# Side jobs of the first attention: scatter and gathers spread over the steps, eight tiles turned at a time, one spare-bank job a step

## The reference, cut to what matters

```
u, v, q, k = split(silu(xn @ W1 + b1), 4)          # 16 heads of 64
av = (silu(q k^T) / 2048) v                        # no softmax: silu of the scores
s  = layernorm(av * u, gamma, beta) @ W2 + b2
```

## Time and profile before

| | us |
|---|---|
| three runs: lowest, median, highest | 4219.31, 4656.99, 4722.14 |
| the profiled execution, its own time | 4205.8 |
| its span (slowest core, core 4) | 4204.2 |
| spans of the eight cores | 4160.4 to 4204.2 |
| TensorE busy in the span | 3919.9 (93%) |
| ScalarE busy | 2097.0 (50%) |
| VectorE busy | 1634.2 (39%) |
| attention of layer 0, core 4 | 129 to 789 |

### The profile page before, as it was taken

One profiled execution on the slowest core, in us unless ns is written; L12 is line 12 of the kernel. 1 busy time (PEld: TensorE's weight loads), 2 busy tenths in 40 slices (PEclk: granted clock), 3 DMA queues, 4 the chain that ended last, 5 costly groups with the idle time before them and its releaser, 6 DMA issues.

```text
span 4204.2 us, 55884 instructions; the slowest of 8 cores (4160.4 to 4204.2 us)
## 1 busy us (share of the span) xinstructions
PE 3919.9 (93%) x20362; PEld 1681.0 (40%) x20362; DVE 1634.2 (39%) x1775; ACT 2097.0 (50%) x2027; POOL 413.6 (10%) x684
## 2 busy tenths in 40 slices
PE   6799777799899999999999999999999999999999
PEld 3333232344444433344443344444344434433444
DVE  6485411002563435333244434424453342355421
ACT  4799757620450556443355554525654553467101
POOL 3000110101110000001100000020000002100000
PEclk9999988999899999999999999999999999999999
DMA  5466865845443349998433333343333334333794
GB/s 157 79 106 109 120 96 105 126 74 152 144 159 128 130 127 220 218 218 212 144 126 123 112 132 117 137 152 113 122 131 124 122 122 145 133 115 119 230 302 143
DMA packets 146591, 593.24 MB, mean 141 GB/s; under 512 B 22517, under 2 KB 49429, under 8 KB 102677
## 3 DMA queue, kind: packets, MB, share of 16 engines
q0 software_dynamic: 80960, 448.84, 41.5%
q1 hardware_dynamic: 65370, 140.83, 10.3%
HBM read 637.80 MB, written 120.63 MB: 180 GB/s over the span
## 4 chain that ended last, share of the span: by engine, by line
PE 76%; DMA 8%; ACT 8%; issue 4%; DVE 3%; DVEq 2%; POOL 0%; SPq 0%; ACTq 0%; POOLq 0%
PE psP L1697 37%; PE psP L1663 10%; PE psP L1719 5%; ACT pt L786 4%; PE psP L1465 3%; PE psP L1413 3%; PE psP L929 3%; PE psP L987 3%; PE psP L1291 2%; DMA w2s<-W 2%; PE psP L291 2%; DVEq L153 1%; PE psP L779 1%; PE psP L312 1%; DMA wsl<-h2wt 1%
## 5 line engine op out<-in xcount | busy, mean ns | idle before, releaser
L1697 PE MATMUL psP<-hB,wsl 128*128 128x512 bf16 x4096 | 923.3, 382 | 23.1 <-DMA wsl<-h2wt 14.2
L1697 PE MATMUL psP<-hA,wsl 128*128 128x512 bf16 x4096 | 928.8, 381 | 3.7 <-DVE nrm L1337 3.7
L1489 DVE TENSOR_TENSOR accs<-accs,pt 128x2048 f32<-128x2048 f32 x192 | 440.1, 2292 | 897.7 <-ACT pt L1480 897.6
L1697 PEld LDWEIGHTS psP<-hB,wsl 128*128 128x128 bf16 x4096 | 393.9, 98 | 524.5 <-issue 77.4
L1697 PEld LDWEIGHTS psP<-hA,wsl 128*128 128x128 bf16 x4096 | 389.4, 98 | 509.3 <-issue 67.8
L1480 ACT ACTIVATE pt<-psP,nbias 128x1024 bf16<-128x1024 f32 x512 | 542.6, 1111 | 93.6 <-PE psP L1465 86.7
L786 ACT ACTIVATE pt<-psP 128x2048 bf16<-128x2048 f32 x341 | 476.6, 1449 | 80.2 <-PE psP L779 76.4
L1663 PE MATMUL psP<-xn,wsl 128*128 128x512 bf16 x2048 | 452.0, 379 | 3.5 <-ACT sgt L1139 1.8
L1480 ACT ACT_TABLE_LOAD x200 | 256.6, 1283 | 355.8 <-PE psP L1465 338.0
L1704 ACT ACT_TABLE_LOAD x181 | 232.2, 1283 | 259.9 <-PE psP L1697 257.1
L1663 PEld LDWEIGHTS psP<-xn,wsl 128*128 128x128 bf16 x2048 | 199.1, 98 | 242.1 <-issue 7.6
(11 more groups left out here) (229 smaller groups left out, 3243.1 us busy)
## 6 DMA issues: line engine op xcount, KB each, us to landing
wsl<-h1b POOLq DMA_DIRECT2D x125, 1024.0 KB, 5.1
wsl<-h2b POOLq DMA_DIRECT2D x96, 1024.0 KB, 5.1
h1b<-h1wt POOLq DMA_DIRECT2D x32, 1024.0 KB, 11.1
wsl<-h2wt POOLq DMA_DIRECT2D x32, 1024.0 KB, 13.7
h2b<-wsl SPq DMA_DIRECT2D x32, 1024.0 KB, 13.3
wsl<-w1b POOLq DMA_DIRECT2D x96, 256.0 KB, 3.6
wsl<-w2b POOLq DMA_DIRECT2D x96, 256.0 KB, 4.1
wsl<-w3b POOLq DMA_DIRECT2D x24, 1024.0 KB, 5.3
```

Source lines behind the costliest of these rows:

```text
L1489: VI(lambda v, a=a, sl=sl: v.tensor_tensor(accs[:], a[:], pt2[sl][:], OP.add))
L1697: emitter(lambda t, it=it, i=i, b=b, src=src: t.matmul(pb(b), wsl[i][:, it, :], src[:, it, :], start=(it == 0), stop=(it == 31)))
```

## The change

- The last row operation now signals, and the first two tiles of W2 are asked for behind it, ahead of the write of `dest_d`.
- The 16 scatters follow at one a step, each behind a wait of POOL for the matmuls of its step; a `w2_sum` comes after every second one. Before, the eight sums came first, one a step, and all scatters were emitted with the last.
- The eight gathers are emitted one a step in the same way.
- `heavy_turn` transposes eight tiles into the whole of bank 7 and copies 1024 columns at once; there are eight calls instead of 16. The means come after them.
- The loop takes at most one job that uses bank 7 in a step, and none in a step in which a fill used it.

```diff
         for i, f in enumerate(row_ops):
             yield (0.3 if i == 3 else 4.5 if i in (5, 10) else 2.5), 0
             VD()
-            VN(f)
+            (VN if i < len(row_ops) - 1 else VI)(f)
+
+        w2_load(tok(cv))
+        w2_load(None)
...
-        w2_load(tok(cv))
-        w2_load(None)
-        for j in range(8):
-            yield 0, 3
-            yield 2.8, 0
-            w2_sum(j)
-        k_accW[0] = tok(cv)
-        wk("v", k)
-        VI(lambda v: v.tensor_scalar(hdi[:], desti[:], NHEAVY, None, OP.min))
+        yield 0, 8
         wk("g", k)
         qtab = stream("qtab")
         for tt in range(NTT):
+
+            yield 0, 4
+            wk("g", tok(ct))
             qtab.n += 16
             Q["g"].append(lambda g, tt=tt: g.indirect_dma_start(
                 tab_d, bass.IndirectOffsetOnAxis(desti[:, tt:tt + 1], 0), tokid[:, tt:tt + 1], None
                 ).then_inc(qtab.h, 16))
+            if tt % 2 == 1:
+                yield 2.8, 0
+                w2_sum(tt // 2)
+        k_accW[0] = tok(cv)
+        wk("v", k)
+        VI(lambda v: v.tensor_scalar(hdi[:], desti[:], NHEAVY, None, OP.min))
         k_rows = tok(cv)
         wk("y", tok(qtab))
         k = y_words(stream("qr10"), sidx[:], tab_d[0:NHEAVY, :].rearrange("(t p) o -> p (t o)", p=128))
-        yield 0, 16
+        yield 0, 10
         wk("g", k, k_rows)
         wk("g", *[tok(st) for st in qxr])
         qxg = stream("qxg")
         for st in range(8):
+            yield 0, 4
+            wk("g", tok(ct))
             qxg.n += 16
...
         k_gather[0] = tok(qxg)
+        yield 0, 8
+        for c in range(NCH):
+            yield 0.8, 0, 1
+            heavy_turn(c)
         for f in range(2):
             yield 0.7, 0, 1
             w2_mean(f)
-        yield 0, 16
-        for c in range(NCH):
-            for hf in range(2):
-                yield 0.8, 0, 1
-                heavy_turn(c, hf)
...
-    def heavy_turn(c, hf):
+    def heavy_turn(c):
         b = take()
         wk("t", k_gather[0])
-        for i in range(4):
-            (TN if i < 3 else TI)(lambda t, c=c, b=b, i=i, hf=hf: t.transpose(
-                pbh(b)[:, i * 128:(i + 1) * 128], xrg[4 * hf + i][:, c * 128:(c + 1) * 128], eye_bf[:]))
+        for i in range(8):
+            (TN if i < 7 else TI)(lambda t, c=c, b=b, i=i: t.transpose(
+                pbh(b)[:, i * 128:(i + 1) * 128], xrg[i][:, c * 128:(c + 1) * 128], eye_bf[:]))
         k_xrg_read[0] = tok(ct)
         wk("v", tok(ct))
-        VI(lambda v, c=c, b=b, hf=hf: v.tensor_scalar(
-            xrhT[:, c, hf * 512:(hf + 1) * 512], pbh(b)[:, 0:512], vcs("gh", c), None, OP.mult))
+        VI(lambda v, c=c, b=b: v.tensor_scalar(xrhT[:, c, :], pbh(b), vcs("gh", c), None, OP.mult))
...
+        bank_used = False
         while (pair["k"] < len(pair["fl"])
                and pair["done"] <= pair["tot"] * (pair["step"] - 1) / 20.0):
             w, f = pair["fl"][pair["k"]]
+            bank_used = bank_used or w > 0
...
-            elif len(job) > 2 and backlog + job[0] > 1.7:
+            elif len(job) > 2 and (bank_used or backlog + job[0] > 1.7):
                 break
             elif backlog + job[0] > room + 0.6:
                 break
             else:
                 backlog += job[0]
+                bank_used = bank_used or len(job) > 2
```

## The result

The kernel after takes 1.0101 of the time of before, 95% interval 1.0075 to 1.0126: **slower by 1.0%**, where 1.4% less was forecast. The profiled execution took 4264.03 us; forecast were 4146, range 4118 to 4182.

A forecast was written before the change was run, and what follows sets the result against it. Plain steps are bound by ScalarE's Silus, steps with fills by TensorE; between, TensorE waits mostly for VectorE's closes behind W2 loads. 66 us off, 6.5 back: 59.5 from 4205.8 gives 4146 us, range 4118 to 4182.

The forecast's parts named there:

- (a): Step 102: the close of a group stands behind four sums; 14 us, forecast to go.
- (b): Steps 106 to 108: the close stands behind the last sums, a W2 load taking 30.0 us; 23 us, to go.
- (c): Step 112: two means in a fill's step, all through bank 7; 4 us, forecast to go.
- (d): Steps 119 to 126: fill and turns share bank 7 one after the other; 24.6 us, forecast to go.
- (e): Steps 134 and 135: the close stands behind seven centres, 12.5 us; moved near step 160, forecast 3.5 us worse.
- (f): Steps 115 to 117, while the gathers run: about 5 us without known cause, forecast to stay.
- R2: Rival: steps 134 to 150, with the turns, run at half clock, 30 us longer, 4176 us; chance 0.05.
- Sums: W2 sums moved off the closes: 37 us go, 1 us left; small writes the smaller part of the slow load.
- POOL and SP: Scatters one a step on POOL, table read on SP: cost 0, gathers nearly covered before the first turn.
- up to 10 us at turn 0: First turn: a single TensorE wait of that size if the gathers' cover is gone; otherwise cost 0.
- R4: Rival: scatters beside all W2 loads slow them throughout, sums and centres wait 130 us, 4252 us; chance 0.03.
- R3: Rival: centre loads quick and (f) gone too, up to 84 us less 2 off, 4124 us; chance 0.17.

The follow-up runs named there:

- e12: The changed kernel with each scatter writing rows of 64 bytes instead of 4, the kernel of e6 run again for its time; 4140.67 us.
- e10: The kernel before with only the table's layout changed, neighbouring tokens' words 64 bytes apart, scatters still in one burst; ratio 0.9986 to before.
- e4: The changed kernel with each scatter writing rows of 512 bytes instead of 4, into a table of that width; 4156.31 us.
- e11: The changed kernel with no casts in steps 92 to 131, issued from step 132 instead, 4-byte scatters to neighbouring words kept; 4239.5 us.
- e6: The changed kernel with each scatter writing rows of 64 bytes (16 words) instead of 4; 4137.24 us.
- e5: The changed kernel with 4-byte writes kept but the rows of the table 512 bytes apart; 4154.9 us.
- e9: The changed kernel with the 8 KB table and 4-byte writes kept, but neighbouring tokens' words 64 bytes apart; 4150.28 us.
- e13: The kernel of e12 with all 16 scatters handed to POOL together in step 100; 4165.31 and 4172.82 us.
- e2: The changed kernel with no casts issued in steps 97 to 131, those ten issued earlier, from step 62; ratio 1.0048 to before.

## Why the prediction was wrong, point by point

- **(a), right.** Step 102 is 3.6 us on all cores, 15.9 to 18.2 before.
- **(b), right on the order, wrong on the loads.** Steps 106 and 107 are plain again (3.5 us; 4.5 once, on core 2). "14 us of slack against a load of 7.9", for 1 us, failed: the median load to 600 us is 31.5 us. Even in e12, without the conflict, these loads have medians of 14 to 16 us on cores 0 to 3 and the longest 21 to 24, so 7.9 was no measure for loads asked for one by one between casts; step 118 takes 8.5 us on the mean there, 4.6 more than plain.
- **(c) and (d), right.** Turn steps are 3.1 us, means steps 2.8, against the 3.0 forecast; the earlier trace rows had 2.56 us of wait in each. Steps 119 to 135, where (d) and (e) lay, priced at 24.6 + 12.5 on core 4, are 29 us shorter in e12 than before on the mean of the cores, its wait for the gathers counted in.
- **(e), right.** The step behind the centres, 161, is 10.9 to 16.5 us; forecast were 15 of wait near 160. The 20 steps from 150 on are 11.3 us longer on the mean, 2.2 more than the 9.1 us that steps 134 and 135 lay above plain before; 3.5 was forecast.
- **(f)** is gone in the form of the earlier trace rows; in e12 steps 115 to 117 take 3.8 us each. Before, only cores 4 to 6 had it. Its cause was not looked for.
- **R2, no.** The turn steps ran at full speed. The stretch at 0.81 on two cores lies some 600 us later.
- **The step that failed** stands under *Sums* and *POOL and SP*: "the small writes are the smaller part", and the scatters at cost 0. It was read off, where the software queue's packets take 11 us each, and I took these as what a cast packet takes. What I left out was the same figure away from scatters. Packets of the software queue, their MB and their time as a share of 16 engines; before, core 4, 540 to 560 us:

```profile
q0 software_dynamic: 129, 1.98, 83.7%
```

That is 0.837 · 16 · 20 / 1.98 = 135 us of engine time a MB, so 4.4 us for a packet of 32 KB. The earlier trace rows has 2.22 · 16 · 5 / 0.52 = 342. The casts were 2.5 times slower beside the scatters, and that was to be seen before. e10 shows it from the other side: with the words 64 bytes apart and the same casts, the longest load of W2 falls from 32.4 to 14.5 us on core 0, so the small writes were the larger part of it. Now after (core 5, 560 to 650 us) and e12 (core 5, 500 to 560 us), with their scatters and casts alike:

```profile
q0 software_dynamic: 525, 4.41, 75.0%
```

```profile
q0 software_dynamic: 875, 6.15, 79.7%
```

After takes 0.750 · 16 · 90 / 4.41 = 245 us a MB, e12 0.797 · 16 · 60 / 6.15 = 124. So in after every cast that meets a scatter holds its engines for twice the time, the W2 loads queue behind it, and spreading makes it last from step 100 to 118: 157 us from the first scatter to the read of the table (495.1 to 652.7) on core 5, in place of 37 us (505.2 to 541.8) on core 4 before, and the casts of that time are seven (last row below). The scatters end late, the table is read late, and the casts that piled up go out among the gathers: the "up to 10 us at turn 0" became 6 to 38. In e12, without the conflict, step 134 is 3.1 to 9.8: the bound held.

The casts of core 5 in the kernel after, 480 to 660 us (count, duration in ns, first and last start):

```profile
L112 POOL DMA_DIRECT2D h1b<-h1wt x7: 546/552/565, 496.1 to 604.2; - x7
```

The prediction used the rule on turns by whole packets (the Trainium skill, DMA: Bandwidth & Descriptors, section Queues, rings and completion order). No row here shows the turns themselves, nor did the 11 us packets. What the rows show fits it: with cast packets twice as long, the median load of W2 is 31.5 us against 14 to 16. What was wrong was what the prediction put a packet's length down to.

- **R4** (0.03, 4252 us) came true, with a part of its mechanism. Its formula with the measured L of 31.5 gives 4 · 31.5 - 61 = 65 us for the sums; steps 102 to 118 took 126.6 us, 62.4 more than the 64.1 of e4. Its second part, 3L - 19 for the centres, did not come: the scatters are over by then and e12's centres wait as long as after's. In its place came the gathers, 20 us on the mean. What R4 lacked was that, at one scatter a step, it needs the casts (e11). Its argument against, that the load of 30.0 us "had a cast, 16 scatters and a weight load on it", is true and was no argument: in after the scatters find casts queued nearly all the time (the seven of core 5 above take 26.6 to 105.8 us from issue to landing).

With the neighbouring writes taken away the prediction's sum comes out: 4146 forecast, 4137 and 4141 measured in e6 and e12, the range 4118 to 4182 holding e4, e5, e9 and e13 too. (Its list of costs adds up to 83 us, not 84; only R3 and R4 use it, and by 1 us.) The attention gave 645.0 - 591.7 = 53 us on the mean and 67 on core 4, against 59.5.

Left open: what makes packets slower (the engine that writes, or the memory that both write to), and below which distance. No run separates these, and why the clock was at 0.81 on two cores isn't known.

## What to carry to other kernels

Before small scatters are spread out beside other traffic, put the written words 64 bytes or more apart, even by changing the address alone; here this turned a loss of 1.0% into a gain of about 1.5%. When a packet in the trace is slow, divide its time by its bytes and set it against the same queue at another time, before its time is put down to its kind. And spreading transfers out only helps if what they share with others is not shared for longer than before: count how many transfers the new stretch meets, not only the slack of one.

## What was not expected of the hardware

- 4-byte writes to neighbouring words, with casts from DRAM to DRAM in the same software queue, make a 32 KB packet of a cast last about 8 us (245 us a MB) instead of 4. Without casts they make the hardware queue's packets three times as long (194 us a MB against 65, e11). The same writes 512 bytes apart do neither harm (e5). Same writes 64 bytes apart: 4150 us, 64-byte rows: 4137 and 4141, 512-byte rows: 4156, neighbouring words: 4244 and 4264.
- A cast can be 105.8 us from issue to landing while POOL issues the next ones in 0.56 us each. Casts issued up to 470 us, ahead of the scatters, were still being carried out at 570 (e2, core 0).
- The kernel of e6 and e12 is the fastest here: the change as made, with rows of 64 bytes.
